# One negated maximum per score step, over four units in two PSUM banks, in a Flamingo-style gated cross attention and linear-mixing block

## What is computed

```
x = x + tanh(g_xattn) * xattn(layernorm(x), ctx, ctx, ...)
h = layernorm(x)
q, k, v = h @ Wq, h @ Wk, h @ Wv            # 16 heads of 16
scores = einsum('bqd,bkd->bkq', q, k) / sqrt(256)
attn = softmax(scores, axis=-1)              # along the queries
z = einsum('bkq,bkv->bqv', attn, v) @ Wo
z = l2_normalize(l2_normalize(z) @ Wff)
x = x + tanh(g_ffn) * gelu(z)
```

## Time and profile before

| what | value |
|---|---|
| median of 3 runs | 1366.96 us |
| lowest, highest | 1364.44, 1368.77 us |
| span of the profiled execution (first to last instruction) | 1360.8 us |
| one iteration of the loop | 71.1 us |
| first iteration starts, last one ends (us in the span) | about 247, about 1243 |
| PE busy | 93% |
| DVE busy | 82% |
| ACT busy | 76% |

### The profile page before, as it was taken

One profiled execution on the slowest core, in us unless ns is written; L12 is line 12 of the kernel. 1 busy time (PEld: TensorE's weight loads), 2 busy tenths in 40 slices (PEclk: granted clock), 3 DMA queues, 4 the chain that ended last, 5 costly groups with the idle time before them and its releaser, 6 DMA issues.

```text
span 1360.8 us, 35101 instructions
## 1 busy us (share of the span) xinstructions
PE 1259.4 (93%) x10770; PEld 797.9 (59%) x10770; DVE 1115.0 (82%) x3180; ACT 1027.6 (76%) x3398; POOL 192.4 (14%) x130
## 2 busy tenths in 40 slices
PE   4999878999999999999999999999999999999875
PEld 2667556656666565657575656565656566665531
DVE  6986666898979797979797979798989989797864
ACT  5667233787878797979796979787887878787787
POOL 2353120102020202020101101010102020202000
PEclk9999899999999999999999999999999999999987
DMA  8440011606060505151514233332415060604131
GB/s 252 139 157 20 6 40 54 196 15 205 5 202 22 191 33 170 53 170 54 170 54 142 82 123 100 97 126 76 148 49 175 15 204 5 203 20 156 55 125 46
DMA packets 163384, 141.26 MB, mean 104 GB/s; under 512 B 9582, under 2 KB 151055, under 8 KB 163344
## 3 DMA queue, kind: packets, MB, share of 16 engines
q1 hardware_dynamic: 163344, 140.76, 32.4%
HBM read 87.00 MB, written 42.55 MB: 95 GB/s over the span
## 4 chain that ended last, share of the span: by engine, by line
PE 60%; DVE 15%; issue 8%; ACT 1%; DMA 1%; SPq 1%; DVEq 0%; PEld 0%; ACTq 0%; POOLq 0%; POOL 0%; PEldq 0%
PE work L891 16%; PE work L893 15%; PE work L892 15%; PE attended L1439 7%; DVE nm L1722 4%; PE score L1428 4%; PE work L1331 2%; DVE Vpl L1619 2%; DVE l2s L1691 1%; DVE x2S L1685 1%; DVE zb L1758 1%; DVE xTl L1638 1%; PE work L1378 1%; DVE wqTl L1624 1%; DVE qst L1644 1%
## 5 line engine op out<-in xcount | busy, mean ns | idle before, releaser
L1528 ACT ACTIVATE prob<-score,nm 128x256 f32<-128x256 f32 x1024 | 478.4, 500 | 38.1 <-DVE nm L1722 36.4
L1722 DVE TENSOR_REDUCE nm<-score 128x2 f32<-128x512 f32 x512 | 336.5, 680 | 16.9 <-PE score L1428 16.6
L1528 ACT ACTIVATION_READ_ACCUMULATOR prob<-score,nm 128x1 f32 x1024 | 238.5, 233 | 0.0
L1644 DVE BATCH_NORM_STATS2 qst<-work 128x6 f32<-128x128 f32 x512 | 112.2, 283 | 92.1 <-PE work L893 92.0
L1439 PE MATMUL attended<-prob,vsp 128*32 128x256 f32 x2048 | 139.2, 397 | 14.7 <-DVE vsp L1737 14.7
L1428 PE MATMUL score<-qstack,kstack 64*128 64x256 f16 x1024 | 99.6, 279 | 11.6 <-ACT prob L1528 9.6
L1576 POOL TENSOR_TENSOR rq<-qft,mhalf 128x32 f32<-128x32 f32 x16 | 86.8, 5428 | 164.8 <-DVEq L1651 164.8
L891 PE MATMUL work<-woutTh,fvph 128*128 128x256 f16 x384 | 105.2, 274 | 2.0 <-DVE Vpl L1619 1.2
L892 PE MATMUL work<-woutTl,fvph 128*128 128x256 f16 x384 | 104.7, 273 | 0.0
L893 PE MATMUL work<-woutTh,fvpl 128*128 128x256 f16 x384 | 104.7, 273 | 0.0
L891 PE MATMUL work<-wTh,xTh 128*128 128x512 f16 x256 | 97.1, 379 | 4.1 <-DVE xTl L1638 3.1
(11 more groups left out here) (327 smaller groups left out, 3270.8 us busy)
## 6 DMA issues: line engine op xcount, KB each, us to landing
qstack<-parts SPq DMA_DIRECT2D x64, 256.0 KB, 3.8
...
```

The costliest lines, as they stand in the source:

```text
L1528: nc.scalar.activation(prob[:, g % PG, e, j + jj, :], sc[n % SC][:, jj * NQ:(jj + 1) * NQ], ACT.Exp, bias=nm[:, u + jj:u + jj + 1], accum_ ...
L1644: last = nc.vector.bn_stats(qst[:, t, 4 * half + h, :], bank(e)[:, h * DH:(h + 1) * DH])
L1722: nc.vector.tensor_reduce(nm[:, u:u + 2], sc[n % SC][:, :].rearrange("p (u q) -> p u q", q=NQ), AX.X, ALU.max, negate=True).then_inc(max_r ...
```

## The change

The four score tensors of one bank become two of two banks each, with the units addressed as (bank, unit, query). `S` and `X` address the same PSUM places as before. An even `M` step now takes the negated maximum of all four units of its bank pair in one instruction, writes four columns of `nm` and raises `max_ready` by 2. The odd `M` steps are gone from `ORDER` and `TAIL`; nothing else in the lists is moved, so the joint step stands where the even one stood.

```diff
-    sc = [ps(f"score{s}", [P, 512]) for s in range(SC)]
+    sc = [ps(f"score{s}", [P, 2, 2, NQ]) for s in range(SC // 2)]
...
-                            last = nc.tensor.matmul(sc[2 * i + e][:, jj * NQ:(jj + 1) * NQ],
+                            last = nc.tensor.matmul(sc[i][:, e, jj, :],
...
-                        nc.scalar.activation(prob[:, g % PG, e, j + jj, :], sc[n % SC][:, jj * NQ:(jj + 1) * NQ], ACT.Exp,
+                        nc.scalar.activation(prob[:, g % PG, e, j + jj, :], sc[n % SC // 2][:, e, jj, :], ACT.Exp,
...
-                    dve.wait_ge(sc_ready, b * SCORES + n // 2 * 2 + 2 + SC_CREDIT)
-                    u = half(n)[3]
-                    nc.vector.tensor_reduce(nm[:, u:u + 2], sc[n % SC][:, :].rearrange("p (u q) -> p u q", q=NQ),
-                                            AX.X, ALU.max, negate=True).then_inc(max_ready, 1)
+                    dve.wait_ge(sc_ready, b * SCORES + n + 2 + SC_CREDIT)
+                    g, i = n // 4, n % 4 // 2
+                    nc.vector.tensor_reduce(nm[:, 8 * g:8 * g + 8].rearrange("p (e i j) -> p i e j", e=2, i=2)[:, i], sc[i][:],
+                                            AX.X, ALU.max, negate=True).then_inc(max_ready, 2)
```

The first line of `ORDER`, as an example of what leaves the lists:

```diff
-rk V0 qs1 V1 V0.h ldx V0.l S0 qpow V1.h G0 M0 V2 G0.h V1.l X0 M1 a1 V2.h S1 G0.l a1.h V2.l X1 G1 M2 G2 M3 G1.h S2 G2.h
+rk V0 qs1 V1 V0.h ldx V0.l S0 qpow V1.h G0 M0 V2 G0.h V1.l X0 a1 V2.h S1 G0.l a1.h V2.l X1 G1 M2 G2 G1.h S2 G2.h
```

More of the change, by code:

```diff
@@ L952 @@
 ORDER = """
-rk V0 qs1 V1 V0.h ldx V0.l S0 qpow V1.h G0 M0 V2 G0.h V1.l X0 M1 a1 V2.h S1 G0.l a1.h V2.l X1 G1 M2 G2 M3 G1.h S2 G2.h
[L954 to L960, removed]
+rk V0 qs1 V1 V0.h ldx V0.l S0 qpow V1.h G0 M0 V2 G0.h V1.l X0 a1 V2.h S1 G0.l a1.h V2.l X1 G1 M2 G2 G1.h S2 G2.h
+a1.l X2 G1.l G3 qs2 X3 G2.l a0 M4 V3 a0.v G3.h aux R0 X4 ldy G3.l S3 z V3.h G4 G5 X5 P0 V3.l G4.h sqe0 G5.h S4 M6
+V4 X6 G4.l X7 M8 V5 wq G5.l V4.h S5 d0 X8 R1 M10 X9 P1 V4.l V5.h sqe1 S6 X10 fk0 V5.l M12 X11 fk1 E0
+d0.o X12 R2 S7 ldr d1 fk0.h L0 M14 fk1.h X13 fk0.l P2 fk1.l m0.h X14 S8 d2 m0.l X15 M16 d3 d1.o X16 d2.o d4
+m1.h R3 m2.h X17 m1.l d5 m2.l S9 S10 d3.o P3 d4.o m3.h M18 y0 m4.h m3.l X18 d5.o X19 M20 m4.l m5.h X20 m5.l S11
+zT0 y1 M22 zT0.h R4 E1 zT0.f L1 y0.o X21 X22 zT0.l zT1 y1.o X23 S12 fk2 ln1 zT1.h P4 fk2.h zT1.f O0 M24 lpow
+X24 S13 R5 X25 ln2 P5 O0. S14 fk2.l zz0 zT1.l E2 zz1 zz0.h M26 q0 zz1.h zz0.l X26 zz1.l q1 M28 X27 pk0 q0.o
+q1.o pq0 pk0.h X28 pk0.l S15 X29 pk1 M30 X30 pq1 L2 R6 X31 P6 pq0.h R7 pk1.h pq0.l P7 pq1.h pk1.l parts0 O1 E3
 L3 pq1.l O2 O1. parts1 O3 O2. q2 O3. back0 q3 F1 q2.o pv0 q3.o F2 back3 q4 pv0.v back1 q5 q4.o back2 F3 q6 q5.o q7
@@ L976 @@
 TAIL = """
[L977 to L986, removed]
@@ L987 @@
-res +M20 +E1 +X19 +M21 +L1 +X20 +S11 +R4 +M22 +P4 +X21 +M23 +X22 +S12 +M24 +X23 +M25 +X24 +S13 +R5 +M26 +P5 +X25 +M27
-+X26 +S14 +O0 +M28 +X27 +M29 +X28 +S15 +M30 +X29 +M31 +E2 +X30 +L2 +R6 +X31 +P6 +O0. +R7 +P7 +O1 +E3 +L3 +O2 +O1. +O3
+rk S0 S1 V0 M0 qs1 G0 V0.h V1 X0 V0.l qpow G0.h V1.h V2 M2 X1 V1.l V2.h S2 G0.l X2 a1 V2.l G1 a1.h G2 G1.h a1.l
+G2.h G1.l X3 G3 qs2 G2.l a0 G3.h M4 S3 a0.v V3 X4 aux G3.l ldr M6 X5 G4 wq X6 S4 R0 G5 M8 P0 X7 sqe0 V3.h R1
+G4.h P1 V3.l G5.h X8 G4.l S5 V4 G5.l X9 M10 E0 X10 S6 d0 M12 X11 L0 sqe1 V5 X12 d0.o S7 V4.h R2 d1 M14 V5.h
@@ new lines @@
+X13 P2 V4.l ldy X14 S8 V5.l d2 X15 M16 d3 m0.h R3 X16 m0.l P3 X17 d1.o S9 d2.o m1.h d4 m2.h m1.l E1 m2.l d5
+d3.o S10 d4.o y0 m3.h M18 m4.h m3.l d5.o m4.l m5.h X18 m5.l y1 M20 X19 X20 R4 L1 X21 y0.o y1.o O0 ln1 S11 O0.
+P4 M22 lpow S12 X22 ln2 X23 M24 zz0 zz1 zz0.h S13 zz1.h zz0.l X24 zz1.l M26 X25 pk0 X26 R5 pq0 pk0.h pk0.l
+P5 pq0.h X27 pq0.l S14 pk1 M28 E2 parts0 X28 S15 O1 M30 X29 L2 X30 pq1 R6 X31 P6 pq1.h R7 pk1.h pq1.l P7 pk1.l
+back0 E3 O1. parts1 L3 O2 O3 O2. back2 +S0 O3. +S1 +M0 +X0 pv0 F1 +M2 +X1 back3 pv1 F2 +X2 back1 +S2 +X3 pv0.v
@@ L989 @@
++S3 +M4 pv1.v +X4 +R0 +M6 +P0 +X5 +X6 +S4 +M8 +X7 +X8 +S5 +R1 +M10 +P1 +X9 +X10 +S6 +M12 +X11
++X12 +S7 +M14 +X13 +X14 +S8 +M16 +E0 +X15 +L0 +R2 F3 +R3 +P2 +P3 +S9 +M18 +X16 F4 +X17 out +X18 +S10
+res +M20 +E1 +X19 +L1 +X20 +S11 +R4 +M22 +P4 +X21 +X22 +S12 +M24 +X23 +X24 +S13 +R5 +M26 +P5 +X25
++X26 +S14 +O0 +M28 +X27 +X28 +S15 +M30 +X29 +E2 +X30 +L2 +R6 +X31 +P6 +O0. +R7 +P7 +O1 +E3 +L3 +O2 +O1. +O3
 +O2. +O3. +F1 +F2 +F3 +F4 +out
```

## The result

| what | before | after |
|---|---|---|
| median of the runs, side by side on one chip (4 runs each) | 1366.12 us | 1397.35 us |
| lowest and highest after | | 1396.44, 1399.1 us |
| ratio, with its 95% interval | | 1.0239 (1.022 to 1.0258) |
| span of the profiled execution | 1360.8 us | 1394.7 us |
| one iteration of the loop | 71.12 us | 73.14 us |

The changed kernel is 2.4% slower. The forecast was 1390.8 us within 1374 to 1400. The two spans differ by 33.9 us: 14 iterations of 2.02 us are 28.3, the tail adds 5.4, and 0.1 lies ahead of the loop (all three rounded).

What follows compares the result with a forecast made beforehand. PE was taken as nearly always at work, bound by tight hand-overs (DVE bounds the iteration's start); terms sum to 1.63 us an iteration, 22.8 over 14, plus 1.0 tail: 1366.96 + 23.8 = 1390.8 us, range 1374 to 1400.

Steps and rivals of the forecast that it cites:

- (1): M0 to G3, start of the iteration: the joint M0 ends 0.53 us later, but G3 only +0.10 us.
- (2): G4: late X0 delays G3.h on ACT, then G3.l and G4; +0.30 us in all, G3's 0.10 within it.
- (3): S5: the joint M6 delays X6 and X7, which S5 waits for; +0.53 us.
- d4, "comes out even": d4's wait for d1.o, after S5: slack just used up by the 0.83 us of lateness, nothing added.
- (4): P5, waiting for R5 behind M24 and M25 on DVE: the saving counts, -0.07 us.
- (5): q0 late through X24, X25 and O0., +0.27 us; q1 late through zz0.l behind the joint M26, +0.17 more.
- (6): P7: X30 now waits for the joint M30, and X31, R7 and P7 follow; +0.43 us.
- the tail: After the loop: each run of X starts 0.5 us late, mostly hidden; 1.0 us, bounds 0.4 and 2.0.
- Fewer instructions win: Rival: DVE's total work decides and ACT's new waits are hidden; 16 us saved, to 1351 us; chance 0.07.
- Nothing moves: Rival: late X are caught up and PE is the bound anyway; 1367 us within 4; chance 0.08.
- half of it: Rival: G4 and S5 late as worked out, more slack late in the iteration; 11.6 us, to 1379; chance 0.20.
- a maximum across two banks costs more: Rival "worse": dearer than two of one bank, or delays reach the next iteration; 1396 us and above; chance 0.10.

Runs made afterwards that it cites:

- M0 and M6 alone: Only M0 with M1, or only M6 with M7, joint in the loop, against two-bank tensors with all maxima single (71.13 us an iteration): 71.42 and 71.67 us.
- the remedy at M6: Changed kernel with M6 and step z exchanged, so that M6 runs 2.3 us earlier: 1397.88 us, 73.15 us an iteration.
- the four single pairs: Four kernels, one pair joint in the loop (M6, M24, M30 or M0), against all maxima single (71.13 us an iteration): 71.67, 71.67, 71.65, 71.42 us.

## Why the prediction was right, and where it was wrong

Right in sign and range, and in the main in the mechanism; 6.6 us low (1390.8 against 1397.35).

| step of the sum | predicted, us | measured, us |
|---|---|---|
| price of the joint maximum, start to start | 1.13 | 1.13 |
| (1), (2): G3, G4 | 0.10, in all 0.30 | 0.16, in all 0.29 |
| (3): S5 | 0.53 | 0.53 |
| d4, "comes out even" | 0 | 0.15 |
| (4): P5 | -0.07 | 0.01 |
| (5): q0 and q1 | 0.27 + 0.17 | 0.53, all of it at S14 |
| (6): P7 | 0.43 | 0.51 |
| an iteration | 1.63 | 2.02 |
| the tail | 1.0 | 5.4 |

*(1) to (3)* hold to 0.01 us at G4 and S5; G3 is late by 0.16 and not 0.10. They are the two chains that were followed instruction by instruction from rows on all three engines, and the experiments with M0 and M6 alone give 0.29 and 0.54 at the same steps. What the prediction left out is a second cause of nearly the same size beside each: V1.l with a1 for G4, and G5.l behind M8 and M9 for d0. They cost nothing extra, since PE pays for the later of the two only. But by the run in which each maximum releases its own `X`, putting X0 right would not bring G4 back, and the second cause at d0 made the remedy at M6 fail.

*d4.* The prediction saw that d4 and d1.o "come out even" and put nothing. It lost 0.15 us; its first load in the changed kernel:

```profile
642.02 0.10 PEld L891 LDWEIGHTS work<-xTh,Gh 128*128 128x128 f16 x1 [0.25 <-DVE md L1676]
```

An estimate of slack from four or five added steps is good to about a tenth; a place that comes out even should have been carried as 0 to 0.15.

*(4).* The saving of 0.07 us at M24 is not there, and the trace shows why. M24 starts 2.42 us after the ln1 step ahead of it began, and 2.35 before; what it saves in length it loses in its start. The section at the end has more on it.

*(5).* The cause was right, M24's lateness in X24; the place was not. I followed it into O0. and q0, and then zz0.l into q1. But X25, which is as late as X24, also frees the bank pair for S14, and S14 stands ahead of both. It takes 0.59 us there; q0 and q1 are then so late that they add nothing, though q1's load still waits 0.27 us for zz0.l. That 0.44 stood in the sum and 0.53 came is therefore luck: it is not the path that was added up. The row of before that would have told it is S14's weight load, shown above, which already waited 0.42 us for an exponential; I had no row of it. The weight loads of every score step were to be looked at, not only S5's.

*(6).* X30 was to be late by 0.49 us more than S15 and is by 0.57: M30 starts 0.50 us behind S15 and not 0.44, the same effect as at M24.

*The tail* is the term that was mis-sized most: 1.0 us taken, 2.0 as the bound, 5.4 measured. The argument was that a run of `X` starts late but its `S` does not move. ACT's waits in the tail of before and of after, from the first tail step to the end (total, times, longest):

```profile
ACT prob L1528 <- DVE nm L1722: 2.7, 7, 0.6
```

```profile
ACT prob L1528 <- DVE nm L1722: 6.7, 10, 1.0
```

In the last pair's own chain a late `X` does move an `S`, since PE waits there for the `X` two steps back. Against the end of the loop the last pair's X0 is 3.19 us late, X8 3.61, X12 3.98, X20 4.58, X24 5.20, X30 5.77: steps of about 0.4 to 0.6 us, at six hand-overs and not at each of the 16 pairs. From the end of the pair before the last (2.66 us late) to X31 they make 3.1 us. The kernel with two single maxima released together has the same steps, 2.7 us in all; the one where each releases its own `X` has 0.8; the nine profiles of kernels with the old tail have between -1.2 and 0.9. So about 3 us of the tail come from the late release.

The 2.66 us that were there already are not shown to come from the joint maxima. At the same place five of those nine profiles are 1.3 to 1.6 us late, and four 0 to 0.2; the kernel with all maxima single is 1.45 us late in one of its two and not at all in the other. With two maxima released together it is 0.65. One thing that differs is the clock. In the loop the granted clock is 1.00 (2.4 GHz), with PE busy for 68.9 of 71.0 us; in the tail, where PE waits more, it changes between 1.00 and 0.50 (1.2 GHz); after the change it is 1.00 from 1324.0 to 1344.0 us and 0.50 from 1344.3 to 1361.0. The tail before, after, and with two released together (length, busy time, PE clock):

```profile
1242.97:1360.80 117.83, 84.94 (x736) 45.62 (x736) 80.32 (x188) 94.39 (x349) 9.71 (x4) 0.83 0.23 75
```

```profile
1271.42:1394.70 123.28, 87.82 (x736) 46.20 (x736) 78.42 (x156) 94.97 (x349) 9.70 (x4) 0.81 0.22 71
```

```profile
1275.13:1396.00 120.87, 85.43 (x737) 44.27 (x736) 80.35 (x188) 94.66 (x349) 9.71 (x4) 0.83 0.23 73
```

The same matmuls take PE 2.9 us more after the change. The third kernel has the mean clock of before, and its tail is longer by 3.0 us and not by 5.4. How the other 2.4 us divide between clock and waits no run here shows.

P6, where the prediction had looked, shows nothing of all this; its wait is 2.16 us where it was 2.15, and it has only moved:

```profile
1377.64 1.36 PE L1439 MATMUL attended<-prob,vsp 128*32 128x256 f32 x16 [2.16 <-DVE vsp L1737]
```

That a wait is as long as before says nothing about whether its place has moved.

*The sum.* The loop was 5.5 us too low (14 x 0.39), the tail 4.4, and 0.1 lies ahead of the loop: 10.1 us on the span. That the forecast missed by 6.6 only is luck. It put the median 6.2 us above the span, as it was before; after, the two are 2.7 us apart. What lies around the span takes 1.7 to 2.0 us in every run that has both numbers. The rest of the 6.2 was that the profiled execution of the kernel before was a short one.

*DVE's busy time* was to fall by 38 us and fell by 5.1 (1115.0 to 1109.9). That line was wrong twice. The records of neighbours overlap, and the busy time counts an overlap once: counted only up to the next record's start, the maxima take 307.8 us of DVE before and 292.0 after, 15.8 less and not 38. That is 0.60 us for a single one and 1.14 for a joint one, and close to the 256 x 0.07 = 18 us of the real saving. Then 10.7 us come back, because DVE is now idle behind other steps more often, and their last 0.08 us, once under the next record, are counted in full (4.2 us of it at L1631). By the Trainium skill, page "VectorE: DVE Perf Modes", section "The DRAIN you can't avoid", the next op starts only when the pipe has emptied; the section adds that a next op that is not held starts earlier, which the prediction left out. The trace after agrees with the second half: a1.l starts at 621.63 while the joint maximum's record runs to 621.71.

*The rivals.* "Fewer instructions win" is refuted by the sign. Its core is partly real: 0.14 us reach PE at G4 when M2 and M4 are joint and nothing is late, and that is the most that was seen. The advice of "VectorE: DVE Perf Modes", section "Rules for kernel authors" in the Trainium skill, to minimize the op count for chained ops, stands in a row whose advice begins "Don't try to fuse for perf". It does not carry over to these pairs, for neither maximum feeds the other and each half has its own reader; joining them cost 2.4%. "Nothing moves" and "half of it" fall with the four single pairs, of which none is caught up. The kernel with two instructions released together puts an end to "a maximum across two banks costs more": it does not.
